# Last batch's rows sent in four groups ahead of the first two experts' tiles' results, with a new order of work around them

## What is computed

```
x = x + LN(attn(LN(x)))      attn: q,k = LN(x) Wq', LN(x) Wk' (bf16), rotary;
                             o = sum over keys of exp(q.k/16), causal; relu(o*fc1+b) fc2 + b
x = x + LN(ffn(LN(x)))       ffn: logits = h gate + b; the two best of 8 experts, softmax of the two;
                             sum over both of weight * (gelu(h W1 + b1) W2 + b2),  W1 256x1024, W2 1024x256
```

## Time and profile before

| | us |
|---|---|
| median of 3 runs (lowest, highest) | 625.47 (624.44, 625.89) |
| the profiled execution | 628.62 |
| its span, first to last instruction | 626.8 |
| PE busy | 559.9 (89%) |
| DVE busy | 415.6 (66%) |
| ACT busy | 366.1 (58%) |
| POOL busy | 182.6 (29%) |
| mean granted clock of TensorE | 0.982 of 2.4 GHz |

### The profile page before, as it was taken

The page is one execution under the profiler, slowest core; times in us unless marked ns, Lnnn a source line. Parts: engine busy times, 40 slices in busy tenths (PEclk is TensorE's granted clock), DMA queues, the critical chain, the costliest instruction groups (busy, mean ns, idle before and its releaser), DMA issues.

```text
span 626.8 us, 14745 instructions
## 1 busy us (share of the span) xinstructions
PE 559.9 (89%) x4306; PEld 499.4 (80%) x4307; DVE 415.6 (66%) x1293; ACT 366.1 (58%) x836; POOL 182.6 (29%) x153
## 2 busy tenths in 40 slices
PE   2988998987998899999999999899999999999940
PEld 1747373644668899999999989899999999998940
DVE  4789698987987555455554556486489655455476
ACT  4376677774644453644635565684688654553582
POOL 2000054355536622313214213113212312312320
PEclk9999999999999989999999999999999999999985
DMA  8930011633227732323322263473473422322479
GB/s 221 359 127 0 2 69 69 237 136 111 73 101 191 225 51 51 50 34 54 47 43 50 43 170 61 93 244 58 70 235 81 67 36 51 50 34 51 89 201 330
DMA packets 51869, 66.80 MB, mean 107 GB/s; under 512 B 4886, under 2 KB 45308, under 8 KB 51708
## 3 DMA queue, kind: packets, MB, share of 16 engines
q1 hardware_dynamic: 37820, 47.87, 24.2%
q0 software_dynamic: 14016, 18.56, 17.2%
HBM read 38.26 MB, written 28.74 MB: 107 GB/s over the span
## 4 chain that ended last, share of the span: by engine, by line
PE 73%; DVE 9%; ACT 5%; issue 4%; DMA 4%; POOL 2%; another core or an unknown queue 1%; DVEq 1%; SPq 0%; ACTq 0%; POOLq 0%
PE pY L1651 30%; PE pL L1638 28%; PE pP L778 5%; DMA sorted_x<-xrows,slot_i 2%; PE pX L464 2%; DVE z L1795 2%; POOL sorted_x L195 2%; PE pP L881 2%; PE pS L795 2%; ACT probs L666 1%; PE pP L838 1%; PE pT L759 1%; ACT xn L597 1%; DMA x_all<-x 1%
## 5 line engine op out<-in xcount | busy, mean ns | idle before, releaser
L1573 ACT ACTIVATE h<-pL,b_now 128x256 f32<-128x256 f32 x272 | 112.6, 465 | 153.7 <-PE pL L1638 80.8
L542 POOL DMA_INDIRECT sum_y<-y,dest x68 | 107.0, 1573 | 274.8 <-DVE y L1695 262.4
L1668 DVE TENSOR_TENSOR h_lo<-h,h_hi 128x512 fp32r<-128x512 f32 x136 | 93.2, 692 | 112.8 <-ACT h_hi L1579 112.2
L1638 PE MATMUL pL<-xeT_hi,w_lo 128*128 128x256 f32 x544 | 151.6, 279 | 6.5 <-issue 5.7
L1651 PE MATMUL pY<-w_hi,h_lo 128*128 128x256 f32 x544 | 155.1, 285 | 2.5 <-DVE h_lo L1668 1.5
L1651 PE MATMUL pY<-w_hi,h_hi 128*128 128x256 f32 x544 | 151.6, 279 | 0.6 <-issue 0.6
L1651 PE MATMUL pY<-w_lo,h_hi 128*128 128x256 f32 x544 | 151.5, 279 | 0.5 <-issue 0.5
L1638 PE MATMUL pL<-xeT_lo,w_hi 128*128 128x256 f32 x544 | 151.0, 278 | 0.0
L1638 PE MATMUL pL<-xeT_hi,w_hi 128*128 128x256 f32 x544 | 150.9, 277 | 0.0
L1638 PEld LDWEIGHTS pL<-xeT_hi,w_lo 128*128 128x128 f32 x544 | 102.0, 188 | 7.8 <-issue 6.9
L1651 PEld LDWEIGHTS pY<-w_hi,h_lo 128*128 128x128 f32 x544 | 102.8, 189 | 4.5 <-DVE h_lo L1668 2.6
(11 more groups left out here) (284 smaller groups left out, 831.8 us busy)
## 6 DMA issues: line engine op xcount, KB each, us to landing
w_stage<-w SPq DMA_DIRECT2D x16, 1024.0 KB
xt<-sorted_x SPq DMA_DIRECT2D x38, 260.0 KB
sum_y<-fill SPq DMA_DIRECT2D x1, 4352.0 KB, 20.6
w_stage<-sum_y SPq DMA_DIRECT2D x8, 512.0 KB, 6.7
out<-z SPq DMA_DIRECT2D x7, 512.0 KB, 6.4
x_all<-x SPq DMA_DIRECT2D x3, 1024.0 KB, 8.4
sorted_x<-fill SPq DMA_DIRECT2D x8, 260.0 KB
sum_y<-y,dest POOLq DMA_INDIRECT x68, 3.8
```

The source lines that it names most:

```text
L542: pool.indirect_dma_start(out=sum_y, out_offset=bass.IndirectOffsetOnAxis(ap=to[:, i:i + 1], axis=0), in_=rows[:, i, :], in_offset=None, c ...
L1573: a = act.activation(h[:, c, :], pL[:, bk, i * TM:(i + 1) * TM], ACT.Gelu, bias=b1_now[par][:, c:c + 1])
L1638: mm = pe.matmul(pL[:, bk, i * TM:(i + 1) * TM], w[:, 0, col], x[:, k, :], start=(k == 0 and w is lo), stop=(k == KC - 1 and x is xeT_lo))
L1668: dve.tensor_tensor(h_lo[:, cs, :], h[:, cs, :], h_hi[:, cs, :].bitcast(F32), ALU.subtract).then_inc(h_split, 1)
```

## The change

The sends of the last batch are now four groups of four, each waited for until it has landed, and all of them stand ahead of the two tiles' results. The second tile ahead has buffers of its own for its results, its weights and its destinations (`y_second`, `weight_second`, `dest_second`), so DVE needs no word from POOL before it fills `y` for tile 2; `y_left` starts two higher. The same buffers also serve the last tiles of the last expert, through the lists `ys_ahead` and so on.

In the batch loop the two halves of the gate and the copies of the logits stand apart, with score tiles between them. The last batch's `hidden` and `attention_mlp` stand ahead of the placing of batch 2's rows and of the first tile's transposes. The copy h_hi of the tiles ahead moves from DVE to ACT (`high_inner_ahead`). `order_experts` and `plan_order` move ahead of `choose(3)` on DVE, and the split of the second tile's h stands before the last copy of the table. Several `keep_warm` are shorter: 14 to 5, 4 to 6, 18 to 8, 5 to 2.

```diff
-            pool.sem_inc(y_left, ONE)
+            pool.sem_inc(y_left, AHEAD + ONE)
             pool.wait_ge(sums_cleared, 16)
             pool.wait_ge(rows_ready, B)
-            send_rows(pool, B - 1, range(SEND_FIRST[0]))
-            scatter_ahead(pool, 0)
-            send_rows(pool, B - 1, range(SEND_FIRST[0], SEND_FIRST[1]))
-            hold(pool, y_sent, 32, y_left)
-            scatter_ahead(pool, 1)
-            send_rows(pool, B - 1, range(SEND_FIRST[1], SEND_FIRST[2]))
-            hold(pool, y_sent, 64, y_left)
-            send_rows(pool, B - 1, range(SEND_FIRST[2], 2 * TB))
+            for first in range(0, 2 * TB, BURST):
+                send_rows(pool, B - 1, range(first, first + BURST))
+                hold(pool, rows_sent, (B - 1) * BATCH_SENT + (first + BURST) * 16, passed)
+            for g in range(AHEAD):
+                scatter_ahead(pool, g)
...
+            def high_inner_ahead(g):
+
+                act.wait_ge(l2_done, 2 * g + ONE)
+                for bk in range(4):
+                    act.wait_ge(h_ready, 4 * g + bk + 1)
+                    act.activation(h_hi[:, 2 * bk:2 * bk + 2, :], h[:, 2 * bk:2 * bk + 2, :],
+                                   ACT.Copy).then_inc(h_hi_ready, 1)
...
                 take_x3T(j)
-                sum_exps(j + 1, range(TB // 2))
-                take_logits(j)
-                sum_exps(j + 1, range(TB // 2, TB))
+                take_logits(j, 0)
+                sum_exps(j + 1, range(2))
+                take_logits(j, 1)
+                sum_exps(j + 1, range(2, TB))
                 weigh(j)
...
-                score(j + 1, range(TB // 2))
                 pe.wait_ge(qk_ready, (j + 2) * 8)
                 gate_half(j, 0)
+                score(j + 1, range(2))
                 gate_half(j, 1)
-                score(j + 1, range(TB // 2, 6))
+                score(j + 1, range(2, TB // 2))
                 turn_logits(j)
-                score(j + 1, range(6, TB))
-                keep_warm(pP[:, 0, :], 4)
+                score(j + 1, range(TB // 2, TB))
+                if j < B - 2:
+                    keep_warm(pP[:, 0, :], 4)
                 rank(j)
-                keep_warm(pP[:, 0, :], 5 if j < B - 2 else 14)
+                keep_warm(pP[:, 0, :], 5)
+            attention_mlp(B - 1)
             turn_ahead(0)
-            keep_warm(pP[:, 0, :], 4)
-            attention_mlp(B - 1)
+            keep_warm(pP[:, 0, :], 6)
...
             def split_bank(g, bk):
                 cs = slice(2 * bk, 2 * bk + 2)
-                dve.wait_ge(h_ready, 4 * g + bk + 1)
-                dve.tensor_copy(h_hi[:, cs, :], h[:, cs, :]).then_inc(h_hi_ready, 1)
                 dve.wait_ge(h_hi_ready, 4 * g + bk + 1)
...
+            hidden(B - 1)
             place_rows(B - 2)
             dve.wait_ge(busiest_known, 1)
             dve.wait_ge(b2_in, 16)
             e0 = busiest(dve)
-            order_experts()
+            split_ahead(range(3, SPLITS))
+            stats_attn(B - 1)
             save_tag(dve, 0)
-            weigh_rows_ahead(0, e0)
-            hidden(B - 1)
-            split_ahead(range(3, SPLITS))
             lower_rows(dve, 0, pXa[0])
-            stats_attn(B - 1)
...
+            order_experts()
+            plan_order()
             choose(B - 1)
-            plan_order()
             place_rows(B - 1)
-            steer_table()
-            dve.wait_ge(l2_done, 2 + ONE)
-            for bk in range(4):
-                split_bank(1, bk)
...
+            steer_table(split_second)
```

More of the change, by code:

```diff
@@ L1252, in steer_table @@
                                          in1=gcol[:, 1:2], op0=ALU.mult, op1=ALU.add).then_inc(words_ready, 1)
+                between()
                 dve.wait_ge(words_turned, 1)
@@ L1669, in split_bank, with weigh_rows @@
                                   ALU.subtract).then_inc(h_split, 1)
-            def weigh_rows(who, g, dest=dest, weight=weight, left=None):
+            def weigh_rows(who, g, dest=dest[:], weight=weight[:], left=None):
                 dve.wait_ge(y_left, (g if left is None else left) + ONE)
```

47 lines of the change are left out of this document (28 added, 19 removed).

## The result

| | before, us | after, us |
|---|---|---|
| median (lowest, highest), 4 runs each | 624.96 (624.36, 625.89) | 633.74 (633.59, 634.65) |
| the profiled execution, its span | 628.62, 626.8 | 634.65, 632.4 |

The ratio of the medians is 1.0154, with a 95% interval from 1.0132 to 1.0176. The change makes the kernel 8.8 us slower. I had said 623.8, in a range up to 629.5, and the result is outside. What happened is the rival called "the results are late", only larger.

The account below looks back on a forecast made before the run. TensorE held 73% of the chain, and the start of tile 5's first layer set the end. It was to move from 237.78 to 236.1: 628.62 - 1.7 = 626.9, or 623.8 on the median's scale, range 620.6 to 629.5.

Parts of the forecast that it names:

- the results are late: Rival, last batch's sends: waits of 16 instead of 12.3, tile 5 at 241.7, +3.9, 629.4 us; chance 0.20.
- The mark and the 11.34 behind it: Start of tile 5's first layer, 237.78 before, forecast 236.1; tiles behind it keep 11.34 us each.
- Batch loop, -1.65: Batch loop: splitting the gate's halves lets exps fill ACT's idle time, gaining 0.55 us a batch, 1.65 for three.
- gives nothing: Rival, batch loop: exps keep their pace, POOL starts 1.2 earlier, not 2.8, tile 5 at 237.7, no change; chance 0.05.
- Up to the last rows: Between batch loop and last batch's sends: rows ready 2.8 us earlier, POOL starts at 179.85 instead of 182.65.
- Shorter `keep_warm`, no price: PE around the third rank and second tile's layer: fewer warming matmuls cost nothing, since the PE waits there anyway.
- The sends in groups: POOL's last batch: four groups of 4.8 us plus waits of 12.3, 31.5 in all, ending at 211.4.
- From `y_left` to the transposes 5.1: From DVE's tag through SP's load to the PE's transposes of tile 5: 5.1 us, 4.7 with quiet queues.
- Half clock if the PE stands long: PE before tile 5: after a long standstill it works at 1.2 GHz for some 3.4 us, losing 1.8.
- ACT's pause stays: ACT's first loop pass, tile 3: the 5.99 us pause should stay, since the branches do, and costs nothing any more.
- Quiet queues by the packet rule: DMA engines alternate between queues by packet, so a send beside weights takes at most twice its quiet time.
- cheap holds: Rival, last batch's sends: all four waits near 2.3, tile 5 at 233.0 to 234.8, -3 to -4.8; chance 0.15.

Follow-up runs that it names:

- b_loop: Kernel before with only the batch loop's new order of scores, gate halves, logits and exps: 631.97 us, ratio 1.0035 on chip C.
- a_mixed: Changed kernel without holds in the last batch, results back between the sends (6, 2, 8): 619.30 us, ratio 0.9930 on chip A.
- after_again: The changed kernel run once more, unaltered, on chip C: 637.74 us, ratio 1.0140.
- before_again: The kernel before run once more, unaltered, on chip C: 629.27 us, ratio 1.0006.
- a_mixed_warm: a_mixed with the old `keep_warm` counts restored and ten more matmuls before tile 0's transposes: 628.76 us, ratio 0.9990 on chip C.
- b_new_order: Kernel before with only the new sends (four held groups of four, then the results) and the second tile's own buffers: 634.42 us, ratio 1.0141 on chip A.
- a_results_between: Changed kernel with all four holds, but the results placed behind groups 2 and 3: 638.03 us, ratio 1.0129 on chip B.
- a_light_weights: Changed kernel with the loop's expert weight loads cut to an eighth: 632.31 us, ratio 1.0042 on chip B.
- a_two_groups: Changed kernel with two held groups of eight sends in the last batch instead of four of four: 628.68 us, ratio 0.9976 on chip B.
- a_covered: Changed kernel, last batch: eight sends, tile 0's results, hold, four sends, tile 1's results, hold, four sends: 632.45 us, ratio 1.0057 on chip D.
- b_mixed: Kernel before with the second tile's own buffers and no holds in the last batch, results at their old places: ratio 1.0017 on chip B.
- b_mixed_again: b_mixed repeated on chip C: 630.92 us, ratio 1.0028.
- a_mixed_burst8: a_mixed with the first three batches' sends in groups of eight, one hold inside a batch instead of three: 638.01 us, ratio 1.0165 on chip C.

## Why the prediction was wrong, step by step

- **The mark and the 11.34 behind it**: right (242.94 to 254.29).
- **Batch loop, -1.65**: in the undisturbed profile -0.35 a batch for 0.55; in time no gain: 2 us slower on the kernel before (b_loop), and no difference that the runs can tell in a_mixed. The rival "gives nothing" was right, for a reason I did not name.
- **Up to the last rows**: right, and on the low side. `hidden(3)` starts at 140.77 for my 141.7, POOL's first send at 178.77 for 179.85, now released by batch 2's held sends. Tile 2's load came 5.7 earlier (185.66 for 191.39), not 2.1. On chip C POOL's first send is only 0.9 earlier (182.13 in after_again for 183.04 in before_again). The rest of the change is worth 3.6 to 4.6 us alone.
- **Shorter `keep_warm`, no price**: right (a_mixed_warm).
- **The sends in groups: this step failed.** I put the waits at 2.6 + 2.8 + 2.5 + 4.4 = 12.3; they were 4.20 + 2.49 + 6.36 + 3.89 = 16.94. The group that I called quiet, the third, was the one beside the weights: SP issued them at 197.41 and not 199.95, because tile 2 was earlier, and group 3's last send of 199.28 fell behind them. My own figures already put it there: by them group 3 is sent until 199.65 and waits until 202.15, so weights issued at 199.95 fall into its wait. In b_new_order, after_again and a_results_between too it is the third wait that is long (6.12, 5.83, 5.55), with the weights issued at 201.31, 200.51 and 200.59. a_light_weights gives the weights 3.0 to 4.3. Group 1 was 1.6 above my figure, and beside light weights three of four waits were still over 3.5, where I had taken the quiet 2.3 as the base. The sum from POOL's start to the first result was 36.9 for 31.5: 4.6 more of waits, and 0.8 because some sends took 1.14 to 1.34 and not 0.97.
- **Six results spaced 1.9, landing 3.8 to 4.4**: right, 9.4 from 215.68 to 225.07, and 3.83.
- **From `y_left` to the transposes 5.1**: right, 5.06. **Half clock if the PE stands long**: right, 7.79 for 5.46, but undersized: with the transposes (1.11 for 0.45) it cost 3.0 and not 1.8.
- **ACT's pause stays**: wrong for the changed kernel; it is in neither of its profiles. It is back in before_again, at its old place in the third bank of tile 3, and in b_loop one bank later (4.49):

```profile
219.60 0.84 ACT L1573 ACTIVATE h<-pL,b_now 128x256 f32<-128x256 f32 x2 [4.46 <-remote]
```

  It does not belong to ACT's code alone: a_two_groups and a_covered differ from the changed kernel in POOL's part only, and ACT stands 5.63 in the one and 17.32 in the other; and b_new_order, b_mixed and b_mixed_again have the ACT code of the kernel before without the pause. The rule of the Trainium skill (Runtime: NRT & Kernel Launch, Instruction fetch mechanics) that a taken branch to a far target waits for a fetch by DMA would fit pauses of an engine in the first pass through its loop, and that they change with what else the DMA engines carry. No run here shows the fetch as their releaser, and the traces speak against a transfer of that kind at the end of each pause: of the packets that the profile calls instruction, none falls into ACT's pause in a_two_groups (203.53 to 209.16), and the only one in before_again's (215.14 to 219.60) starts at 219.26 and still runs when ACT goes on.
- **Quiet queues by the packet rule**: the Trainium skill (DMA: Bandwidth & Descriptors, Queues, rings and completion order) lets a DMA engine alternate between its queues. I had weighed it as speaking for cheap holds. Here the trace does not decide: 6.36 beside the weights is 2.6 times the 2.49 of group 2, more than the twice that I had drawn from the rule, but only 1.7 times the 3.69 of the same group beside light weights. What the cheap holds needed was four waits near 2.3, and only one was.

The sum itself held: with waits of 16, `y_left` at 229 and a slowed PE, the rival's formula gives 241.7, against 242.94, and the difference is the half clock. Of the 9.9 us between 623.8 and 633.74, 6.8 are the mark (242.94 for 236.1): 3.8 for the late transposes, 3.0 for the half clock. Another 2.2 come from the scale: I took the 3.15 by which the profiled execution of before was long off the sum, and that of the changed kernel was only 0.9 above its median. The last 0.9 lies behind the mark and outside the span. One sum of the rivals is off: for the cheap holds, -3 to -4.8 gives 621.6 on average and not 622.2. What I should have done is price the step by its position relative to events that the same change moves: having moved tile 2 and the weights earlier, I had to move the groups' neighbours too. And my chance of 0.20 for the late results was low for a forecast whose largest term was four waits of which each could be 2.3 or 6.6.

What stays open: what the waits above 2.3 go to when the weights are gone; what the PE's gaps and ACT's pauses wait for, and why they come in some POOL orders and on some chips; and why the new batch order loses time while POOL sends.

## What to carry to other kernels

A wait in an engine's queue costs its full length to whatever stands behind it in that queue: four waits ahead of six results became 17 us, and the place of the results among them did not matter. Before adding such waits, follow the chain from the last thing behind them to the bottleneck engine, and compare its arrival with the engine's need, at both ends of the wait's range. And the reverse: a wait that looks like pure loss may serve something; one hold inside a batch instead of three cost 12 us in the batch loop, and the runs do not say by what.

## What the runs showed of the hardware

- Where the next expert's 2 MB of weights are issued while four row sends are under way, POOL waits 5.55 to 6.36 for them to land, and 3.69 with an eighth of the weights.
- Eight row sends in a row instead of four made the kernel 12 us slower, and both batches beside which POOL sends 3 us longer (37.1 and 37.7 for 34.05; the first of them took up to 37.8 with groups of four too), although the share of the DMA engines beside the weight loads was the same (0.94 and 0.95).
- An engine can pause with nothing to wait for that the profile shows. In the first pass through its loop ACT stood 4.46 to 5.99 in before, before_again and b_loop, 5.63 in a_two_groups, 6.75 in a_mixed_burst8 and 17.32 in a_covered. The PE lost 2.2 to 4.4, in single steps of up to 1.9, in the kernels without holds on chips B, C and D and in a_two_groups. None of these is in the four profiles of chip A, though the DMA share was 0.94 there too.
- A clock of 0.67 over 9 us, raised to 1.00 by warm matmuls, brought no time: from there to the mark it was 92.7 and 92.8 us.
